# Block products for all four chunks from tile 5 on, weight chains from unit 8, and filler matmuls in the opening

## What is computed

```python
x = L0_attn_u                                   # (4, 512, 512): 2048 tokens of 512 features
x = x + attn(layernorm(x)) + ffn(layernorm(x))

# attn: an S4 layer. K is made from a sum over 64 states at 512 roots of unity, then
y = irfft(rfft(u, 2L) * rfft(K, 2L), 2L)[..., :L] + D[0] * u      # L = 512

# ffn: weights of 4-bit codes, a table of 16 values and a scale for each 64 codes
Wg, Wu, Wd = dequant(gate), dequant(up), dequant(down)            # 1792 x 512, 1792 x 512, 512 x 1792
h = silu(x @ Wg.T) * (x @ Wu.T)
out = h @ Wd.T
```

## Time and profile before

| | us |
|---|---|
| median of 3 runs (lowest, highest) | 471.56 (471.34, 473.03) |
| the profiled execution | 473.78 |
| span of its core | 472.0 |
| PE busy | 449.4 (95%) |
| DVE busy | 376.8 (80%) |
| ACT busy | 275.3 (58%) |
| POOL busy | 182.7 (39%) |

### The profile page before, as it was taken

The page is one execution under the profiler, slowest core; times in us unless marked ns, Lnnn a source line. Parts: engine busy times, 40 slices in busy tenths (PEclk is TensorE's granted clock), DMA queues, the critical chain, the costliest instruction groups (busy, mean ns, idle before and its releaser), DMA issues.

```text
span 472.0 us, 7230 instructions
## 1 busy us (share of the span) xinstructions
PE 449.4 (95%) x2598; PEld 254.7 (54%) x2598; DVE 376.8 (80%) x605; ACT 275.3 (58%) x468; POOL 182.7 (39%) x181
## 2 busy tenths in 40 slices
PE   0789999999999999999999899999999999999997
PEld 0544444443444444444444344456544688888886
DVE  5879869987677687875886676864999899999993
ACT  8947565586767866567674865863332533544340
POOL 0552589503275653746557474666200000000000
PEclk9989999999999999999999999999999999999999
DMA  8372536112425234212231225235790021001111
GB/s 283 84 278 67 113 62 169 47 46 89 156 67 179 89 140 151 69 44 89 68 90 56 80 42 152 89 94 171 227 340 3 1 92 46 15 32 46 46 46 45
DMA packets 31832, 47.21 MB, mean 100 GB/s; under 512 B 13044, under 2 KB 14132, under 8 KB 31284
## 3 DMA queue, kind: packets, MB, share of 16 engines
q1 hardware_dynamic: 30516, 42.56, 29.3%
q0 software_dynamic: 1280, 4.20, 2.8%
HBM read 35.93 MB, written 8.72 MB: 95 GB/s over the span
## 4 chain that ended last, share of the span: by engine, by line
PE 65%; DVE 4%; DMA 4%; ACT 3%; issue 2%; POOL 2%; SPq 0%; DVEq 0%; POOLq 0%; ACTq 0%
PE bank L2196 20%; PE bank L1949 15%; PE bank L2090 15%; PE bank L2147 8%; PE bank L2137 6%; DMA lines<-wd 3%; POOL work L818 1%; ACT work L887 1%; ACT work L872 1%; DMA work<-in_q_down 1%; DVE work L1227 0%; DVE h L1348 0%; DVE work L1231 0%; DVE h L1291 0%; PE bank L2039 0%
## 5 line engine op out<-in xcount | busy, mean ns | idle before, releaser
L1949 PE MATMUL bank<-xT,w 128*128 128x512 f16 (+1 forms) x732 | 166.5, 380 | 1.9 <-DVE w L1241 1.7
L887 ACT ACTIVATE work<-work 128x512 f32<-128x512 int32 (+1 forms) x186 | 104.7, 621 | 36.7 <-POOL work L818 33.1
L1949 PEld LDWEIGHTS bank<-xT,w 128*128 128x128 f16 x732 | 72.3, 99 | 87.3 <-DVE w L1241 2.1
L818 POOL TENSOR_SCALAR work<-work 128x512 f32<-128x512 int32 x31 | 64.4, 2078 | 31.2 <-DVE work L1207 16.7
L2196 PE MATMUL bank<-wd,work 128*128 128x256 f16 x504 | 56.2, 273 | 0.0
L2196 PEld LDWEIGHTS bank<-wd,work 128*128 128x128 f16 (+1 forms) x504 | 49.3, 98 | 6.0
L831 POOL TENSOR_SCALAR w<-work,sc 128x512 f16<-128x512 f32 x17 | 28.3, 1664 | 55.3 <-DVE work L1231 55.2
L2090 PE MATMUL bank<-h 128*128 128x512 f16 x198 | 48.1, 379 | 1.5 <-DVE h L1291 1.5
L1167 ACT ACTIVATE work<-h 128x896 f16<-128x896 f32 x30 | 27.9, 943 | 28.4 <-DVE h L1857 18.3
L2196 PE MATMUL bank<-h,work 128*128 128x256 f16 x378 | 42.2, 273 | 0.0
L2196 PEld LDWEIGHTS bank<-h,work 128*128 128x128 f16 x378 | 37.0, 98 | 4.3
(11 more groups left out here) (192 smaller groups left out, 642.8 us busy)
## 6 DMA issues: line engine op xcount, KB each, us to landing
h<-in_x SPq DMA_DIRECT2D x8, 512.0 KB, 4.9
moved<-h SPq DMA_DIRECT2D x4, 1024.0 KB, 4.7
xT<-in_x POOLq DMA_DIRECT2D x16, 256.0 KB, 4.0
h<-moved SPq DMA_DIRECT2D x4, 1024.0 KB, 10.8
out<-xT SPq DMA_DIRECT2D x15, 256.0 KB, 2.1
work<-in_q_gate SPq DMA_DIRECT2D x14, 256.0 KB, 2.8
work<-in_q_up SPq DMA_DIRECT2D x14, 256.0 KB, 2.6
work<-in_am_gate SPq DMA_DIRECT2D x28, 128.0 KB, 3.0
```

The costliest lines, as they stand in the source:

```text
L818: pool.tensor_scalar(chain_room(u, "r"), qs[:, u % 2, :], RIGHT_FROM, RIGHT_FROM, ALU.max, ALU.subtract).then_inc(first_done, 1)
L887: nc.scalar.activation(room, qs[:, u % 2, :] if j == 0 else room, KNEE, scale=scale, bias=bias, alpha=below).then_inc(knee_done, 1)
L1949: mm = nc.tensor.matmul(out_b, weights(k)[:, unit, wl, f, :], xT[:, TPC * c + first:TPC * c + last, xl, f, :], start=(i == 0), stop=(i == ...
```

## The change

- `FIRST_BLOCKED = (3, 4)`: side 0 (chunks 2 and 3) is blocked from tile 3 as before, side 1 (chunks 0 and 1) from tile 4. Each side has its own banks A, E, B (4, 5, 6 and 0, 1, 2), semaphores and token sums. Chunk 2 and chunk 0 have the role B (silu of the gate in bank A, up in bank B), chunks 3 and 1 the role E. The four sums of token blocks of side 1 that add hi and lo are made by POOL (`token_whole`), the rest by DVE and ACT in windows 3 and 4.
- The window of PE has a new order: P1 of both sides, P4 of the tile before for both sides, P5, P6, P2, P3, P7 of both. DVE's window begins with the second joins and the h of the tile before. ACT's window has `part(0, 3)`, `copy_m1` of side 0, `part(3, 4)`, `copy_m1` of side 1, both `copy_m5`, and so on.
- hi of h of chunk 0 is made by POOL from tile 4 on (`h_hi(k)`), in the loop of units, ahead of the first hi half of the next window.
- `CHAINED = range(7, UNITS)`: units 7 to 10 are chained too, and all their hi halves are POOL's (`POOL_HALVES = CHAINED`).
- `EARLY_IN = (5, 6, 9, 12)`: four rows of down in the windows instead of six; five units instead of three lie in the convolution.
- POOL's small steps of exp and V no longer stand ahead of the units but between them (`small_steps`).
- `MOVED = 6`; the residual x is reloaded by SP instead of POOL.
- PE: three runs of products of the identity into bank 2, which nobody reads: 8 ahead of the first transposes, 6 behind the fourth, 4 behind the fifth.

```diff
+ROLE_B, ROLE_E = (2, 0), (3, 1)
+FIRST_BLOCKED = (3, 4)
+A_BANK, E_BANK, B_BANK = (4, 0), (5, 1), (6, 2)
...
-EARLY_IN = (5, 6, 9, 10, 11, 12)
+EARLY_IN = (5, 6, 9, 12)
...
-DOWN_ROWS = (0, 1, 2, 3, 4, 12, 5, 6, 7, 8, 9, 10, 11, 13)
-CHAINED = range(11, UNITS)
-POOL_HALVES = range(CHAINED[0], UNITS - 4)
+DOWN_ROWS = tuple(range(NM))
+CHAINED = range(7, UNITS)
+POOL_HALVES = CHAINED
...
-MOVED = 4
+MOVED = 6
...
+            def small_steps(u):
+
+                if made_before(3) <= u < made_before(4):
+                    for i in range(0, 9) if u == made_before(3) else range(9, EXP_STEPS):
+                        exp_step(i)
+                elif made_before(4) <= u < made_before(5):
+                    for i in range(0, 5) if u == made_before(4) else range(5, 10):
+                        v_step(i)
+                elif u in (made_before(7), made_before(7) + 1):
+                    for i in range(10, 15) if u == made_before(7) else range(15, V_STEPS):
+                        v_step(i)
+            def h_hi(k):
+
+                pool.wait_ge(h_done, H_COUNT[NCH * k])
+                pool.tensor_copy(hs[:, HOME[k], HI, :], sil[:, 0, :]).then_inc(hhp_done, 1)
...
-            pool.wait_ge(v_done, V_STEPS)
             first_pass(CHAINED[0])
+            first_pass(CHAINED[1])
+            for i in range(4):
+                token_whole(i)
             for u in POOL_HALVES:
-                first_pass(u + 1)
+                if CHAINED[1] < u + 1 < UNITS:
+                    first_pass(u + 1)
+                for k in range(4, NM):
+                    if u == (made_before(k + 1) if k < NM - 1 else TAIL - 1):
+                        h_hi(k)
+                if u == UNITS - 1:
+                    pool.wait_ge(conv_done, NT)
                 weight_hi(u)
                 gate_copy(u)
+                small_steps(u)
                 if u == made_before(NM - 3) - 1:
                     turned_rows()
...
@@ ACT @@
             def window(k):
                 n = NCH * k
+                if HOME[k] != k:
+                    act.wait_ge(moved_st[HOME[k]], 16)
+                part(k, 0, 3)
+                copy_m1(0, k)
+                part(k, 3, 4)
+                copy_m1(1, k)
+                copy_m5(0, k)
+                copy_m5(1, k)
+                part(k, 4, 6)
+                silu(n + 2)
                 silu(n)
+                part(k, 6, 7)
+                silu(n + 3)
+                part(k, 7, 8)
                 silu(n + 1)
+                if k + 1 < NM:
+                    block_hi(k + 1, 0)
+                    block_hi(k + 1, 1)
...
@@ DVE @@
             def window(k, stage=None):
+                n, both = NCH * (k - 1), k > FIRST_BLOCKED[1]
+                join(0, k - 1, 1)
+                h_mul(n + 3)
+                if both:
+                    join(1, k - 1, 1)
+                h_mul(n + 1)
+                block_lo(k, 1)
...
+                h_mul(n + 2)
+                stage_of(0, 2)
+                if both:
                     h_mul(n)
+                stage_of(2, 5)
+                if both:
                     h_lo(n)
...
+                join(0, k, 0)
+                stage_of(5, 6)
+                join(1, k, 0)
+                stage_of(6, 8)
+                if k + 1 < NM:
+                    other_sums(k + 1)
+                    block_lo(k + 1, 0)
...
@@ PE @@
             def blocked_window(k):
+                for s in sides(k):
+                    blocked_product(s, k, 1)
+                for s in sides(k - 1):
+                    blocked_product(s, k - 1, 4)
+                for s in sides(k):
+                    blocked_product(s, k, 5)
+                for s in sides(k):
+                    blocked_product(s, k, 6)
+                for s in sides(k):
+                    blocked_product(s, k, 2)
+                for s in sides(k):
+                    blocked_product(s, k, 3)
+                for s in sides(k):
+                    blocked_product(s, k, 7)
...
+            warm_up(8)
             turn(0)
             turn(1)
...
             turn(3)
+            warm_up(6)
...
             turn(4)
+            warm_up(4)
             turn(5)
```

More of the change, by code:

```diff
@@ L1110, in _, with part, first_window @@
             items(ACT_AT[8] + 1, ACT_AT[9] - 3)
+            def part(k, first, last):
+                items(eighths(ACT_AT, k, first), eighths(ACT_AT, k, last))
+            def first_window(k):
+                n = NCH * k
+                silu(n)
+                items(ACT_AT[9] - 3, ACT_AT[9])
+                copy_m1(0, k)
+                h_hi(n)
+                copy_m5(0, k)
+                part(k, 0, 2)
+                token_hi(1, 0)
+                part(k, 2, 3)
+                silu(n + 2)
+                part(k, 3, 5)
+                silu(n + 1)
+                token_hi(1, 1)
+                part(k, 5, 6)
+                silu(n + 3)
+                part(k, 6, 8)
+                block_hi(k + 1, 0)
+                block_hi(k + 1, 1)
+                token_hi(1, 2)
+                token_hi(1, 3)
@@ L1112, in window @@
             def window(k):
                 n = NCH * k
-                if k == NM - MOVED:
-                    act.wait_ge(moved_st, 16 * MOVED)
-                def part(first, last):
-                    items(eighths(ACT_AT, k, first), eighths(ACT_AT, k, last))
-                silu(n)
-                copy_m1(k)
-                if k > BLOCKED[0]:
-                    part(0, 2)
-                h_hi(n)
-                copy_m5(k)
-                if k == BLOCKED[0]:
-                    items(ACT_AT[9] - 3, ACT_AT[9])
-                    part(0, 2)
@@ L1144, in _ @@
+            first_window(3)
+            for k in range(4, NM):
                 window(k)
-            items(ACT_AT[made_before(NM - 1) + LAST_UNITS], ACT_AT[UNITS])
-            weight_hi(UNITS - 1)
+            items(ACT_AT[TAIL - 1], ACT_AT[UNITS])
             def sum_hi(s, i):
@@ L1321, in join, with token_lo @@
-            def join(k, i):
-                m5 = h_place(k, 3)
+                v.tensor_tensor(made, one, two, ALU.subtract).then_inc(xs_done[s], 1)
+            def token_lo(s, i):
+                dve.wait_ge(xs_hi[s], TOKEN_LO[s][i])
+                hi, lo = (tk[s][:, i, l].rearrange("p f t -> p (f t)") for l in (HI, LO))
+                v.tensor_tensor(lo, x_sums[s][(1, 2, 0, 3)[i]], hi, ALU.subtract).then_inc(xs_lo[s], 1)
+            def join(s, k, i):
+                m5, n = h_place(k, ROLE_E[s]), k - FIRST_BLOCKED[s]
@@ L1574, in _ @@
             h_mul(6)
-            items(33, 37)
+            items(33, 35)
+            items(35, 36)
             h_mul(7)
@@ L1596, in _, with first_window @@
             block_lo(BLOCKED[0], 1)
-            items(41, 42)
-            items(43, 45)
-            def window(k, stage=None):
+            def first_window(k):
                 def part(first, last):
                     items(eighths(DVE_AT, k, first), eighths(DVE_AT, k, last))
+                n = NCH * k
+                part(0, 2)
+                token_sum(1, 0)
+                h_mul(n)
+                token_sum(1, 1)
+                h_lo(n)
+                part(2, 4)
+                join(0, k, 0)
+                token_sum(1, 2)
+                part(4, 6)
+                token_sum(1, 3)
+                part(6, 8)
+                other_sums(k + 1)
+                block_lo(k + 1, 0)
+                token_lo(1, 0)
@@ L1604, in stage_of, with window @@
+            def window(k, stage=None):
                 def stage_of(first, last):
                     for slot in range(first, last):
-                        part(slot, slot + 1)
+                        items(eighths(DVE_AT, k, slot), eighths(DVE_AT, k, slot + 1))
                         if stage:
                             stage(slot)
-                n = NCH * k
-                if k == NM - MOVED:
-                    dve.wait_ge(moved_st, 16 * MOVED)
-                if k == BLOCKED[0]:
+                n, both = NCH * (k - 1), k > FIRST_BLOCKED[1]
[5 more added lines that the diff above has]
+                block_lo(k, 1)
+                if not both:
+                    token_lo(1, 1)
+                h_mul(n + 2)
+                stage_of(0, 2)
+                if both:
@@ L1638, in _ @@
+                stage_of(6, 8)
+                if k + 1 < NM:
+                    other_sums(k + 1)
+                    block_lo(k + 1, 0)
+            first_window(3)
+            for k in range(4, NM - 7):
                 window(k)
@@ L1793, in _ @@
             window(NM - 1, stage=kernel_stage)
-            at = made_before(NM - 1) + LAST_UNITS
-            items(DVE_AT[at], DVE_AT[at + 1])
-            at, per = DVE_AT[at + 1], DVE_AT[UNITS] - DVE_AT[at + 1]
+            n = NCH * (NM - 1)
+            for s in range(2):
+                join(s, NM - 1, 1)
+            h_mul(n + 3)
+            h_mul(n + 1)
+            h_mul(n + 2)
+            h_mul(n)
```

(3 more changed lines are left out.)

527 lines of the change are left out of this document (292 added, 235 removed).

## The result

The changed kernel took **528.02 us** (526.85 to 529.48, 4 runs) where the kernel before took 471.56 (471.34 to 473.03): a ratio of **1.119**, 95% interval 1.1155 to 1.1228. It is slower, as forecast, but by 56.5 us where 16.9 were forecast, and it lies beyond the range of 468 to 503.

The account below looks back on a forecast made before the run. PE's own work was taken to set the time. Terms -12.95 - 3.6 (old stalls) - 1.4 + 18.0 + 10.0 + 1.0 + 4.5 + 1.4 = +16.95 us gave a forecast of 488.5 us, chance 0.60, range 468 to 503.

Parts of the forecast that it names:

- PE's work: Tiles 4 to 13, chunks 0 and 1: 60 fewer matmuls at 216 ns each, -12.95 us.
- The opening: Unread products in PE's opening gaps keep the clock, so the first product takes 2.75 us, not 4.15: -1.4 us.
- Five three-unit windows: Windows 5, 6, 9, 12, 13: P6 waits for copy_m1 behind a pass needing POOL's first pass; 3.6 us each, +18.0.
- Windows 3 and 4: POOL's token sums and small steps between units delay window 4's join and P6: +10.0 us (5 to 14).
- Window 7: Five V steps stand ahead of the first pass that ACT wants before two silus: +1.0 us (0 to 2).
- Window 11: POOL's turned_rows copies wait for DVE's quarter turns, delaying P6 of side 0: +4.5 us (3 to 5).
- Clock behind long stalls: Seven stalls of 3 us or more could each lower PE's clock; one drop taken, +1.4 us (0 to 9.8).
- The tail: Two more units lie in the convolution, but residual loads go to SP and the tail still runs on PE: 0.
- rival (c): Two-unit windows stall as well, 1 us in each of five, and the clock falls each time: over 500 us; chance 0.10.
- Rival (a): PE stays the bound, faster: the window stalls vanish, 453.6 us, or 456 with a few small ones; chance 0.19.

Follow-up runs that it names:

- the kernel with all the mends: Changed kernel with copies, third units' first pass and residual loads earlier, turned_rows and block_lo later, small steps regrouped, side 1's token sums on VectorE: 470.18 us, 0.9945.
- the best kernel: The kernel with all the mends, with window 3's VectorE sums and differences spread around the join and GpSimd's cast behind the high half: 467.42 us, 0.989.
- the kernel with all copies ahead: Changed kernel with all four ScalarE copies of a window (copy_m1 and copy_m5, both sides) ahead of chain passes part(k, 3, 4): 511.52 us, 1.081.
- the kernel with the copies and GpSimd's first pass ahead: The kernel with all copies ahead, plus GpSimd's first pass of the third unit ahead of the first unit's high half in three-unit windows: 511.06 us, 1.083.

## Why the prediction was right or wrong, point by point

- **PE's work, -12.95 us:** right. In the kernel with all the mends two-unit windows take 18.13 us (189.64 to 207.77), the hand-timed value. This gain of 13 us was always there, and the changed kernel lost 74 us beside it (44.2 idle, 19.9 slow, 10.0 behind the windows).
- **The opening, -1.4:** the trace of the changed kernel has the product at 2.75 us, but the step was wrong: one slow product in one execution was taken as a property of the kernel. Measured worth: 0 (ratio 1.0003), and with the filler the product was slow in three of 19 profiles.
- **Five three-unit windows, +18.0:** the mechanism was right, link by link. In window 6 (start 168.97) GpSimd and ScalarE show it:

```profile
176.28 1.60 POOL L893 CAST h<-work 128x512 f16<-128x512 f32 x1 [7.01 <-DVE work L1473]
177.87 1.57 POOL L923 TENSOR_SCALAR w<-work,sc 128x512 f16<-128x512 f32 x1
179.52 2.49 POOL L910 TENSOR_SCALAR work<-work 128x512 f32<-128x512 int32 x1
```

```profile
182.04 0.63 ACT L981 ACTIVATE work<-work 128x512 f32<-128x512 f32 x1 [6.42 <-POOL work L910]
182.58 0.58 ACT L1067 ACTIVATE bank<-bank 128x512 f32<-128x512 f32 x1
```

  The sixth product began 14.2 us into the window, not 12.9: VectorE's chain was 0.6 later, and the first pass took 2.49 us, not the 1.93 of the earlier trace rows. Idle time 25.2 us for 18.0.
- **Windows 3 and 4, +10.0:** mis-sized. Idle time was 13.5 us there (range 5 to 14), and some 5 us of slow matmuls came on top. The step that failed is "the lo half of unit 7 at 93, about when PE wants it". The duration of GpSimd's sums was well bounded (2.56 us for 2.8), but what they do to VectorE was left out: it was slowed to 11.2 us where 3.9 were due, and the lo half came at 97.4. Chain steps of exp were priced rightly (nine took 5.4 us for 5.8).
- **Window 7, +1.0:** no stall. **Window 11, +4.5:** idle time 4.54 us; worth 6.8 alone and 4.1 beside the other mends.
- **Clock behind long stalls, +1.4 (0 to 9.8):** the largest error. The slow matmuls in the windows make 19.9 us in the trace, another 3.3 stand behind them. The step that failed was the choice of one drop in seven, though the opening's row had shown a fall behind a wait of 1.0 us. All eight stalls of 4.3 us or more have slow groups behind them. A drop was priced at 1.4 us, the loss of one group of twelve, while PE stayed below full clock for 4 to 6 us; the filler gave back 2.2 us for each of the four drops that it kept off, and the eight make some 2.5 each (19.9 over eight). The Trainium skill (TensorE: Matmul & The Clock Gate, Part 1) says that an idle array falls to half rate, and was quoted for the upper half only; by it each of the seven stalls would have been counted as a drop, and the trace has eight.
- **The tail, 0:** wrong, 10.0 us (6.7 idle, 3.3 at a lower clock). The step that failed is "the residual loads go to SP": they were taken off GpSimd's bill, and their new queue wasn't read. They stand on SyncE behind two code loads, which wait for rooms that ScalarE and GpSimd free late. Worth 9.5 and 8.1 in two settings. Nothing of it hung on VectorE's amount of work, which the prediction had counted.
- **Sum:** of the 39 us by which the forecast fell short, 18.5 are the clock in the windows (19.9 for 1.4), 10.0 the tail and 10.7 idle time (44.2 us for 33.5); the opening's 0.5 goes the other way. The rival (c), over 500 us with a clock that falls each time, was the case that came, with a chance of 0.10; its other half, stalls in two-unit windows, did not (0.64 us at most in 7, 8 and 10).
- **Rival (a), 453.5 to 456:** even with the orders mended the best kernel takes 467.4, since windows 3 and 4 keep some 9 us above PE's work.

## What to carry to other kernels

In a chain that runs through three or four in-order queues the worth of a mend depends on the others: single mends gave 0 to 18 us, and one that gave nothing alone gave 16 us as the last. So mend all orders that a trace names, then take each out again to learn its price. When you time a change by hand, count for each stall of some us the matmuls at the low clock behind it as well, and ask of each operation that changes its engine whom it slows there and what stands ahead of it in its new queue.

## What the runs showed of the hardware

- **Stalls and the clock.** Every PE stall of 4.3 to 6.8 us in the changed kernel's windows was followed by matmuls at about the 1.2 GHz level, six of 512 columns in about 2.7 us for 1.47. Shorter ones went both ways. In the kernel with all copies ahead a stall of 2.24 us had a slow group behind it (4.44 us for 2.75), and one of 2.23 us had hardly any (2.91). The widest pair is one of 1.57 us with a slow group, in the kernel with the copies and GpSimd's first pass ahead, and one of 3.92 us with none, in the changed kernel with the sums on VectorE:

```profile
247.93 4.44 PE L2263 MATMUL bank<-h,w 128*128 128x512 f16 x12 [1.57 <-DVE h L1450]
```

```profile
121.30 1.46 PE L2271 MATMUL bank<-h,w 128*128 128x512 f16 x6 [3.92 <-DVE h L1456]
```

  Unread matmuls in the stall kept the clock up in four windows of five; in the fifth the groups behind them had a clock of 0.63 over 4.0 us (157.6 to 161.6).
- **GpSimd beside VectorE.** While GpSimd added two inputs (2.56 us for 1024 columns), VectorE's operations with two inputs took 2.4 us for 0.74 and 3.1 for 1.25; while VectorE ran such operations back to back, four sums among them, a one-input operation of GpSimd took 8.50 us for 1.57. The Trainium skill (SBUF — State Buffer, Who interferes with whom) says that the two share a pair of ports under an exclusive lock, and that a VectorE instruction with two inputs from SBUF contends with a GpSimd instruction that reads SBUF. These rows agree: each slowed VectorE operation took 1.7 to 1.9 us longer, less than one GpSimd sum, and GpSimd's took 6.9 us longer.
- **Two levels of one program.** The kernel before itself runs mostly at about 471.6 or 473.3 us from one execution to the next, with a mean clock of 1.00 in most of the lower and 0.996 in most of the upper ones. A gain of 0.3% can't be read from one profile of it.
